# A LayerNorm's mean as products of rounded high and low parts, with new due times

## What is computed

```python
xn = _layernorm(x, axis=-1)
s = _L0_attn_ref(xn, Wq, Wkv_down, Wk_up, Wv_up, Wout)        # causal attention, 16 heads, latent of 64
g = _silu(_L0_ffn_ref(xn, wqkv, q_scale, k_scale, wo, ln_g, ln_b, w1, b1, w2, b2))
x = x + s * g
```

```python
h = shift_token(x)                     # second half of the features from the token before
q, k, v = split(h @ wqkv)              # 8 heads of 64
q, k = rotary_xpos(l2norm(q) * qs, l2norm(k) * ksc)
x = x + local_attention(q, k, v) @ wo  # window 128: own block of keys and the one before
h = shift_token(x)
mu = h.mean(-1, keepdims=True)
var = h.var(-1, keepdims=True)
h = (h - mu) / jnp.sqrt(var + 1e-05) * lg + lb
a, g = jnp.split(h @ w1 + b1, 2, axis=-1)
x = x + (a * gelu(g)) @ w2 + b2
```

## Time and profile before

| | |
|---|---|
| median of 3 runs | 2777.76 us (2777.74 to 2779.83) |
| profiled execution | 2770.4 us |
| its span, first to last instruction | 2768.5 us |
| TensorE busy in the span | 2555.4 us (92%) |
| DVE, ACT, POOL busy | 1777.0, 1494.4, 1653.5 us |
| mean granted TensorE clock | 0.973 |

### The profile page before, as it was taken

How to read it: one execution, slowest core, us unless ns; L and a number is a source line. 1 busy time by engine, 2 the same in 40 slices (tenths; PEclk the granted TensorE clock), 3 DMA queues, 4 the chain that set the end, 5 groups by cost and what they waited for, 6 DMA issues and landing times. The chain is left out here.

```text
span 2768.5 us, 45326 instructions
## 1 busy us (share of the span) xinstructions
PE 2555.4 (92%) x17264; PEld 1706.4 (62%) x17264; DVE 1777.0 (64%) x3208; ACT 1494.4 (54%) x2039; POOL 1653.5 (60%) x1471
## 2 busy tenths in 40 slices
PE   5799999999999999999995799999999999989996
PEld 3577777777777777777774455545554555445543
DVE  4678677777778777777741575646564675556661
ACT  3257776677765777666762344443444453443443
POOL 2477666666666666676651155664467465754575
PEclk8799999999999999999997799999999999999998
DMA  7110010010111100000000100000000000000000
GB/s 260 48 34 29 12 31 28 28 37 22 39 37 48 37 14 26 28 30 29 17 15 21 65 1 24 8 1 31 17 15 1 12 20 31 1 1 24 24 1 8
DMA packets 68434, 79.93 MB, mean 29 GB/s; under 512 B 11048, under 2 KB 52348, under 8 KB 67196
## 3 DMA queue, kind: packets, MB, share of 16 engines
q1 hardware_dynamic: 68220, 77.03, 8.8%
HBM read 56.04 MB, written 20.97 MB: 28 GB/s over the span
## 5 line engine op out<-in xcount | busy, mean ns | idle before, releaser
L1629 ACT ACTIVATE g_pt<-ps 128x1024 f32<-128x1024 f32 x288 | 293.7, 1020 | 481.3 <-PE ps L1499 481.3
L1833 POOL TENSOR_TENSOR g_total<-g_total,g_pt 128x1024 f32<-128x1024 f32 x168 | 399.9, 2381 | 140.0 <-ACT g_pt L1629 134.7
L1737 DVE TENSOR_REDUCE g_most<-ps 128x2 f32<-128x1024 f32 (+3 forms) x256 | 261.7, 1025 | 99.8 <-PE ps L1468 95.4
L1513 PE MATMUL ps<-g_pt,g_latV 128*64 128x512 f32 x1152 | 310.3, 617 | 0.0
L1830 POOL TENSOR_TENSOR g_total<-g_pt 128x1024 f32<-128x1024 f32 x56 | 133.5, 2384 | 289.7 <-ACT g_pt L1629 262.4
L1468 PEld LDWEIGHTS ps<-g_lat_hi,g_q_hi 64*128 64x128 f32 x768 | 73.3, 184 | 228.8 <-issue 80.5
L1468 PE MATMUL ps<-g_lat_hi,g_q_hi 64*128 64x512 f32 (+3 forms) x768 | 165.9, 425 | 43.4 <-DVE g_q_lo L1717 19.1
L1213 POOL TENSOR_TENSOR l_act_lo<-l_u,l_act_hi 114x512 fp32r<-114x512 f32 x96 | 124.1, 1293 | 127.1 <-ACT l_act_hi L941 127.0
L1041 DVE CUSTOM_DVE_ANT_0 ps<-ps,l_mask 128x256 f32<-128x256 f32 (+1 forms) x512 | 190.5, 440 | 12.7 <-PE ps L677 11.9
L1733 DVE TENSOR_TENSOR ps<-ps,g_mask 128x256 f32<-128x256 f32 x256 | 109.0, 426 | 118.7 <-PE ps L1468 118.7
L1099 DVE SCALAR_TENSOR_TENSOR l_u<-ps,l_b,l_u 114x512 f32<-114x512 f32 x96 | 70.6, 749 | 171.2 <-ACT l_u L931 139.1
(11 more groups left out here) (241 smaller groups left out, 7257.9 us busy)
## 6 DMA issues: line engine op xcount, KB each, us to landing
l_tab<-turns SPq DMA_DIRECT2D x64, 128.0 KB, 2.2
f_xtok<-in_L_attn_x_bld_dram SPq DMA_DIRECT2D x4, 1024.0 KB, 13.5
xnorm<-f_xT SPq DMA_DIRECT2D x4, 1024.0 KB, 5.3
l_xw<-xnorm SPq DMA_DIRECT2D x8, 512.0 KB, 4.3
mid<-l_xw SPq DMA_DIRECT2D x8, 512.0 KB, 3.3
l_xw<-mid SPq DMA_DIRECT2D x8, 512.0 KB, 4.3
state<-l_xw SPq DMA_DIRECT2D x8, 512.0 KB, 3.1
g_xn<-xnorm SPq DMA_DIRECT2D x8, 512.0 KB, 4.3
```

Source lines behind the costliest of these rows:

```text
L1513: last = pe.matmul(ps[64 * a:64 * a + 64, BPV, :], latV[:, units[u][0] % 2, k, :], PT[:, i % NPT, a, :], start=(i == first[u]), stop=(i == ...
L1629: act.activation(PT[:, i % NPT, :, :], ps[:, BST:BST + 2, :], ACT.Exp).then_inc(s["ex"], 1)
L1737: dve.tensor_reduce(to, ps[:, bank:bank + 2, 0:n], AX_X, ALU.max, negate=True).then_inc(s["mx"], 1)
L1833: pool.tensor_tensor(to, to, here, ALU.add).then_inc(s["sum"], 1)
```

## The change

The chunk after the residual is split before the mean: a new event `halve` copies it to `l_h_hi` on ACT and subtracts on POOL into `l_h_lo` (tiles that otherwise hold the normalised chunk, written later). The mean is then four matmuls, a matrix of 1/256 in fp32r (`l_oner`, copied once on DVE) times the high and times the low parts. 1/256 is exact in that type. All due times of the five engines are replaced, of which one line is shown for each of two engines.

```diff
-        "pe": {"bias": (-27.37, 2, 4.02, 5.59), "proj": -2.57, "val": -2.41, "turn": -1.1, "scores": (-0.78, -0.73),
...
+        "pe": {"bias": (-34.64, -0.24, 1.66, 5.68), "proj": -2.63, "val": -2.52, "turn": -1.31,
...
-        "pool": {"split": -2.64, "norm": -1.57, "step": (1.06, 1.33), "divide": 1.89, "var": 5.7, "centre": 5.75,
...
+        "pool": {"split": -3.27, "norm": -1.92, "step": (0.36, 0.41), "divide": 1.27, "var": 5.22, "centre": 5.26,
+               "gate": (6.01, 6.35, 6.36, 6.71, 6.96, 7.11), "halve": 4.49},
...
+        oner = sb("l_oner", [P, P], F32R)
...
                 def mean(q, bank):
-                    pe.wait_ge(s["xw"], KD * (q + 1))
-                    pe.wait_ge(s["xcol"], q + 1)
-                    for k in range(KD):
-                        last = pe.matmul(ps[:, bank, :], ones[:, :], shifted[:, k, :], start=(k == 0), stop=(k == KD - 1))
+                    pe.wait_ge(s["oner"], 1)
+                    pe.wait_ge(s["mlo"], q + 1)
+                    for part in (hh, hl):
+                        for k in range(KD):
+                            last = pe.matmul(ps[:, bank, :], oner[:, :], part[:, k, :], start=(part is hh and k == 0),
+                                             stop=(part is hl and k == KD - 1))
                     last.then_inc(s["mean"], 1)
...
+                def halve(q):
+                    act.wait_ge(s["xw"], KD * (q + 1))
+                    act.wait_ge(s["xcol"], q + 1)
+                    if q:
+                        act.wait_ge(s["upa"], HT * q)
+                    act.activation(hh[:, :, :], shifted, ACT.Copy).then_inc(s["mhi"], 1)
...
+                dve.tensor_copy(oner[:, :], ones[:, :]).then_inc(s["oner"], 1)
...
+                def halve(q):
+                    pool.wait_ge(s["mhi"], q + 1)
+                    pool.tensor_tensor(hl[:, :, :], shifted, hh[:, :, :], ALU.subtract).then_inc(s["mlo"], 1)
```

More of the change, by code:

```diff
@@ L395 @@
         "sp": {
-               "bring": (-50.02, -27.03, -12.94, -10.67, -6.28, -3.66, 2.52, 3.58, -11.97, -7.69, -6.39, -4.62, -3.9, -2.75, -0.65, 0.4, 1.25, 1.95, 2.54, 4.22),
-               "load": -6.38, "xload": 1.56, "store": 5.04},
-        "pe": {"bias": (-27.37, 2, 4.02, 5.59), "proj": -2.57, "val": -2.41, "turn": -1.1, "scores": (-0.78, -0.73),
-               "shift": -0.48, "step": (0.76, 0.8), "weigh": 1.34, "total": 1.38, "wo": 5.17, "mean": 5.26,
-               "var": 5.39, "centre": 5.43, "up": (5.98, 6.04, 6.42, 6.73, 7.18, 7.18),
-               "down": (6.89, 6.92, 7.74, 7.86, 7.92, 8.01)},
@@ L402 @@
-        "act": {"split": -2.33, "proj": -1.96, "norm": -1.33, "val": -1.85, "turn": -0.71, "shift": -0.01,
-               "step": (1.28, 1.3), "total": 1.86, "divide": 2.23, "mean": 5.71, "var": 5.89, "centre": 6.08,
-               "up": (6.31, 6.57, 6.98, 7.16, 7.42, 7.5), "gate": (6.71, 6.82, 7.23, 7.36, 7.79, 8.21)},
-        "dve": {
[L406 to L409, removed]
@@ L410 @@
-        "pool": {"split": -2.64, "norm": -1.57, "step": (1.06, 1.33), "divide": 1.89, "var": 5.7, "centre": 5.75,
-               "gate": (6.35, 6.68, 6.97, 7.11, 7.56, 7.64)},
+               "bring": (-62.66, -47.02, -39.16, -38.75, -31.67, -26.41, -3.19, 0.81, -8.98, -5.79, -4.9, -4.8, -0.66, -0.4, 0.24, 0.37, 0.92, 2.4, 3.39, 4.54),
+               "load": -5.39, "xload": 3.18, "store": 6.58},
+        "pe": {"bias": (-34.64, -0.24, 1.66, 5.68), "proj": -2.63, "val": -2.52, "turn": -1.31,
+               "scores": (-0.96, -0.86), "shift": -0.56, "step": (0.53, 0.58), "weigh": 1.18, "total": 1.29,
+               "wo": 4.83, "mean": 5.35, "var": 5.4, "centre": 5.49, "up": (5.69, 5.88, 5.95, 6.73, 6.78, 7.02),
+               "down": (6.88, 6.97, 7.5, 7.68, 7.76, 7.83)},
@@ new lines @@
+        "act": {"split": -2.47, "proj": -1.94, "norm": -1.28, "val": -1.87, "turn": -0.54, "shift": -0,
+               "step": (1.3, 1.48), "total": 1.94, "divide": 2.29, "mean": 5.76, "var": 5.97, "centre": 6.27,
+               "up": (6.49, 6.56, 6.75, 7.48, 7.51, 7.67), "gate": (6.65, 6.86, 7.47, 7.52, 7.61, 8.17), "halve": 5.73},
+        "dve": {
+               "bring": (-42.62, -37.6, -29.49, -20.37, -4.75, -0.91, 4.54, 5.69, -2.71, -2.57, -2.38, -2.38, 1.82, 2.09, 4.04, 4.24, 5.18, 5.65, 6.61, 7.4),
+               "bias": (-16.26, 0.85, 2.5, 6.41), "scores": (-0.15, -0.1), "peak": -0.05, "proj": -1.66, "turn": -0.47,
+               "total": 2.14, "wo": 5.56, "mean": 5.86, "centre": 6.2, "up": (6.65, 6.84, 6.99, 7.56, 7.65, 7.83),
+               "out": 8.56},
@@ L518, in layers @@
                        "ctx chi clo wo xw xcol mean hc hsq var ve vl vr vn vn2 vn3 rs rsb hn hhi hlo upg upa ge u uhi ulo "
-                       "dn y out whi wlo wb biased")
+                       "dn y out whi wlo wb biased mhi mlo oner")
         def place_of(g):
@@ L961, in _ @@
                         divide(e[1])
+                    elif e[0] == "halve":
+                        halve(e[1])
                     elif e[0] == "mean":
```

## The result

The changed kernel takes **2811.0 us** (median of 4 runs, 2804.9 to 2814.4), the kernel before 2777.8 (4 runs, 2775.9 to 2779.8): ratio 1.0117, 95% interval 1.0097 to 1.0138. So it is slower, as forecast, but by 33 us and not by 13, and 3 us above the top of the range, 2808.

A forecast was written before the change was run, and what follows sets the result against it. TensorE was taken to bound the layers, with the LayerNorm chain just touching it. Chunks +12.8, start +6 and -2.5, second-layer biases -5, end +2.7 summed to +14 us: 2791 us against the median of 2777.76, range 2764 to 2808.

The forecast's parts named there:

- TensorE's work and the walk to up: LayerNorm in each chunk: mean 0.96 us shorter on TensorE, yet up starts later, +1.75 us a chunk with that saving included.
- POOL's share in it: Peaks' cast on DVE again meets POOL's line 1164 through the shared ports, so shift is ready at 10.9 us, not 10.2.
- The give-back: Later in a chunk: rotary-product waits and some shift waits go, 0.9 us a chunk returned, leaving net +0.85.
- clean chunks multiplied by 15: Layers: net +0.85 us a chunk taken for 15 chunks, +12.8 us, bounds +1 to +26.
- the moved weight splits on DVE: Second layer's weight splits, moved on DVE: cost nothing under the wait for the late mean, 1.5 us each without that cover.
- the biases' -5 us: Second layer: both biases move in front of a turn and the late up, saving 5 us, bounds 0 and -6.
- Start: Before the first projection: pieces 8 and 9 ahead of the tokens cost +6 us; moving bias 0.1 gives -2.5.
- the -2.5 for bias 0.1: Start: bias 0.1, which cost 2.46 us, moves behind turn 1, where TensorE sat idle 4.01 us.
- End: Last chunk, nothing beside the chain: 1.06 + 2.38 + 0.2 us more for copy and subtraction, 0.96 less for the mean, +2.7.
- A: Rival: TensorE's work alone decides, up does not wait for the low half; 2752 us, chance 0.1, another 0.1 for half.
- B: Rival: effects cancel, the chain costs 1.75 us a chunk but 1.7 come back, biases give 6; 2779 us, chance 0.2.
- D: Rival: halve delays POOL's norm until after centre has started, so nothing comes back; 2805 to 2812 us, chance 0.15.

The follow-up runs named there:

- The order alone: Only the new due times, with the old fp32 mean at the new place and no halve, against the kernel before: 2811.5 us (ratio 1.0129).
- the fillers: Changed kernel plus unread matmuls of constants: 3 ahead of the mean's wait in odd chunks, 3 before shift, 5 ahead of first up: 2803.4 us (ratio 1.0100).

## Why the prediction was wrong, point by point

- **TensorE's work and the walk to up: right.** Mean 1.01 us for 0.96, up at 17.94 for 18.0, +1.70 us a chunk for 1.75, all in chunks with the full clock. The order alone delays up by the same 1.75, so that the 0.96 us saved never had a chance to count. POOL's share in it is right too: the cast of 8 columns took 1.86 us (0.43 in the earlier trace rows) and the shift came at 10.83.
- **The give-back: right in kind, somewhat low.** 1.2 us instead of 0.9. The waits for the rotary products went, the longest shift wait (1.71 us now) stayed, as the prediction had it. In sum the shift waits of chunks 1 to 13 grew to 23.0 us, because of the new one of 0.77 us behind the variance. Net +0.5 us in a clean chunk, +6 or 7 over 14, where +0.85 was forecast.
- **The step that failed first: clean chunks multiplied by 15.** The sum has no term for TensorE's clock. The prediction knew of new waits, the one ahead of up alone put at 2 us a chunk, but not that short waits can lower the clock; 9 more stretches at 1.2 GHz cost about 10 us, shown by the fillers.
- **The second: "the moved weight splits on DVE I cost at nothing, they run while DVE waits for the late mean".** DVE was waiting, but POOL was in the halve, and a cast beside it took 2.72 us; chunk 6 is 2 us longer than without halve. Chunks 5 to 8 are 6.8 us further over the clean ones than before, and about half of that is clock. The wait in chunk 7 that also stands without halve has an open cause, and no trace shows the biases' -5 us.
- **Start: +6 - 2.5 predicted, +8.5 measured.** The +6 was right. Counted from the start of the layers, which lay 2.7 us later in this trace, the tokens were issued at 14.3 us (14.5 predicted) and the projection came at 19.5 (19.6 predicted, 13.5 before). What failed is the -2.5 for bias 0.1: it did fill a wait, but new waits of 2.42 us for a tile's low half and 2.06 for the peaks came behind it, and the rest of the stage took 2.5 us more.
- **End: +2.7 predicted, +5.4 measured.** The "0.96 less" for the mean held only for a busy TensorE; here mean and variance ran at a granted clock of 0.50, and the variance took 3.55 us instead of 2.63. Chunk 14, counted as an ordinary one, lost 3.8: its trace has no projection or value beside its chain, and up started at 19.37 instead of 16.06.
- **Sum.** The misses in the traces: clock +10.5; turn and biases +11.5 (6.5, what is left of the middle, instead of -5); start +5; chunk 14 +3; end +2.7; the varying first line 2.7; rest 0.7; clean chunks about -6. That is +30, the difference between 44 and 14.
- **The rivals.** A and B were wrong in their mechanism: up does wait for the low half. D has the measured time within its 2805 to 2812, but by chance: its way did not come about, since the norm did not get later than centre, and the give-back did come.

## What to carry to other kernels

A chain that only just touches the engine that bounds the kernel should not get longer, even if the engine has less to do for it: 0.96 us of TensorE were saved a chunk, and 1.7 us lost before any give-back. Where a change adds short idle times to TensorE, look at the granted clock of a chunk of the trace, and give it a term of its own; a few matmuls of constants in the right gaps test that within one run. Look at it also for every chunk that is to serve as the clean one: of the even chunks of the run with the order alone, only chunk 0 was. And price a step that is moved by what runs on the neighbouring engine in its new place, not only by whether its own engine is idle there.

## What was not expected of the hardware

TensorE was busy 1084 of 1139 us and its clock still fell 11 times. Most falls came behind waits of 0.8 to 0.9 us ahead of mean and shift, or behind one of 1.84 us ahead of up, but the same waits also passed without a fall. With all of them filled it stayed up, but for three stretches in chunks 7 and 8; with the last alone filled it fell 11 times as before. Between 280 and 1430 us each fall of the changed kernel lasted 3.4 us and cost 0.75 to 1.6 us. A DVE cast 128x768 took 0.55 to 0.58 us with no large POOL operation beside it, and 2.45 to 2.72 beside one of 128x1024, the halve or one of the norm's.
